# A mixture-of-experts tower on one core: 17 expert tiles listed ahead of the other 22, and the token permutation moved from TensorE's operands to VectorE

## The reference

```python
h = take(W.T, x) + b + positions                    # embedding
u = layernorm(h)
Bu = einsum(u, B_bar)                               # 64 complex states
xs = associative_scan(x_t = Lambda_bar * x_(t-1) + Bu_t)   # along a sequence
h = h + gelu(2 * real(einsum(xs, C_tilde)) + D * u)
v = layernorm(h)
logits = v @ router_w.T + router_b                  # 8 experts
w, e = softmax(top_k(logits, 2))
y_e = (silu(v @ fc1a_e.T + b1a_e) * (v @ fc1b_e.T + b1b_e)) @ fc2_e.T + b2_e
out = h + w_0 * y_(e_0) + w_1 * y_(e_1)
```

## Time and profile before

| | us |
|---|---|
| median of 3 runs | 197.66 |
| the profiled execution | 196.35 |
| its span, first to last instruction | 194.6 |
| PE busy / PE weight loads busy | 126.1 / 105.5 |
| DVE busy / ACT busy / POOL busy | 124.0 / 72.0 / 90.5 |

### The profile page before, as it was taken

How to read it: one execution, slowest core, us unless ns; L and a number is a source line. 1 busy time by engine, 2 the same in 40 slices (tenths; PEclk the granted TensorE clock), 3 DMA queues, 4 the chain that set the end, 5 groups by cost and what they waited for, 6 DMA issues and landing times.

```text
span 194.6 us, 3493 instructions
## 1 busy us (share of the span) xinstructions
PE 126.1 (65%) x784; PEld 105.5 (54%) x784; DVE 124.0 (64%) x478; ACT 72.0 (37%) x230; POOL 90.5 (46%) x117
## 2 busy tenths in 40 slices
PE   0000493969967948835230999999999999995000
PEld 0000323929826817715230888889888988894000
DVE  1838979599997498344530277777777677762082
ACT  2010633181271131141000665666556655663000
POOL 6787850000077375373671045556555565556100
PEclk9999998795896695765555599999999999999555
DMA  4221275050061061011012223333341011100493
GB/s 117 69 54 42 54 153 131 0 163 0 5 203 55 31 216 41 14 56 44 27 55 55 68 60 86 104 99 84 89 111 56 32 40 42 41 33 20 136 398 115
DMA packets 13445, 15.57 MB, mean 80 GB/s; under 512 B 3027, under 2 KB 9437, under 8 KB 13426
## 3 DMA queue, kind: packets, MB, share of 16 engines
q1 hardware_dynamic: 9474, 8.17, 15.8%
q0 software_dynamic: 2784, 5.28, 8.2%
q10 hardware_dynamic: 1168, 1.90, 2.8%
HBM read 9.53 MB, written 6.27 MB: 81 GB/s over the span
## 4 chain that ended last, share of the span: by engine, by line
PE 43%; DVE 26%; issue 14%; DMA 6%; POOL 4%; ACT 3%; DVEq 0%; POOLq 0%; SPq 0%; ACTq 0%
PE bank L902 8%; PE bank L908 7%; PE bank L918 7%; PE bank L791 5%; PE bank L894 4%; PE bank L793 4%; PE bank L792 4%; POOL sorted_rows L320 3%; PE bank L920 2%; DVE zst L486 2%; DMA yres<-results 2%; DVE ysum L635 1%; DVE res L638 1%; DVE zin L485 1%; DVE zrot L489 1%
## 5 line engine op out<-in xcount | busy, mean ns | idle before, releaser
L330 POOL DMA_INDIRECT results<-ysb,dest x39 | 38.4, 984 | 38.9 <-ACT ysb L737 24.4
L320 POOL DMA_INDIRECT sorted_rows<-rows,slot x32 | 31.3, 977 | 44.8 <-DVE slot L533 36.3
L608 DVE SCALAR_TENSOR_TENSOR act_h<-bank,bias_t,sil 128x128 f32<-128x128 f32 x78 | 23.8, 347 | 16.3 <-PE bank L908 15.9
L599 DVE COPY w1b<-w_sb 128x512 f32 x39 | 24.2, 621 | 11.9 <-issue 11.9
L717 ACT COPY xT<-bank 128x128 f32<-128x128 f32 x39 | 10.4, 266 | 43.1 <-issue 21.6
L902 PE MATMUL bank<-xT,w1b 128*128 128x128 f32 x156 | 24.9, 284 | 0.0
L725 ACT ACTIVATE sil<-bank,bias_t 128x128 f32<-128x128 f32 x78 | 24.4, 364 | 0.9 <-PE bank L902 0.9
L908 PE MATMUL bank<-xT,w1b 128*128 128x128 f32 x156 | 24.4, 280 | 0.0
L918 PE MATMUL bank<-w_sb,act_h 128*128 x156 | 23.9, 276 | 0.1
L902 PEld LDWEIGHTS bank<-xT,w1b 128*128 128x128 f32 x156 | 23.4, 212 | 0.3 <-issue 0.3
L908 PEld LDWEIGHTS bank<-xT,w1b 128*128 128x128 f32 x156 | 21.3, 198 | 0.0
(11 more groups left out here) (191 smaller groups left out, 215.7 us busy)
## 6 DMA issues: line engine op xcount, KB each, us to landing
w_sb<-w_all SPq DMA_DIRECT2D x8, 384.0 KB
xt<-sorted_rows SPq DMA_DIRECT2D x39, 65.0 KB, 1.9
yres<-results SPq DMA_DIRECT2D x4, 256.0 KB, 4.4
yres<-results ACTq DMA_DIRECT2D x4, 256.0 KB, 4.9
results<-ysb,dest POOLq DMA_INDIRECT x39
sorted_rows<-pad SPq DMA_DIRECT2D x1, 520.0 KB, 5.9
sorted_rows<-rows,slot POOLq DMA_INDIRECT x32
out<-res SPq DMA_DIRECT2D x2, 256.0 KB, 2.5
```

The source lines that it names most:

```text
L320: gp.indirect_dma_start(sorted_rows[:, :], bass.IndirectOffsetOnAxis(ap=slot[:, k, t:t + 1], axis=0), rows[:, k, t, :], None).then_inc(s_s ...
L330: gp.indirect_dma_start(results[:, :], bass.IndirectOffsetOnAxis(ap=dest[:, i:i + 1], axis=0), ysb[i][:, :], None, bounds_check=bound, oob ...
L599: v.tensor_copy(w1b[i % 3][:, :], w_sb[:, bass.ds(at, 2 * HID)]).then_inc(s_wb, 1)
L608: v.scalar_tensor_tensor(act_h[i % 2][:, q], ps_l[i % 2][:, q], bias_t[:, 2 + c, i:i + 1], sil[i % 2][:, q], ALU.add, ALU.mult).then_inc(s ...
```

## The change

1. **Two lists of tiles.** Once three of the four groups have been sorted, 24 tiles' worth of rows are there, and at least 24 - 7 = 17 full tiles of 128 rows whatever the routing is. `EARLY` = 17 such tiles get their own table (`early_counts`, `early_owners`, `early_table`, `early_bias`), which waits for nothing of group 3. SP loads them when the scatters of groups 0 to 2 have landed (`s_scat` is now one semaphore per group). The other 22 tiles (`LATE`) get theirs afterwards (`late_table`), from the full counts less what the first list has done. The scatter of an early tile's result takes its row numbers straight from `xt`.
2. **Token permutation on DVE.** `turn_u` writes its tiles side by side, `outputs` reads `zrot` and `uT` without a step, and DVE's four multiplications in `scan(g)` read PSUM (L510 and L512 of the changed kernel) or write SBUF (L519, L520) with a step of 128 elements instead.
3. **Start.** `root_h` is set among POOL's first constants, and ACT fills `decay` after it has copied `bbarT`.

```diff
-CHUNKS = [0, 2, 4] + list(range(8, NTILES, 4)) + [NTILES]
+EG = 3
+EARLY = EG * GT * K - (NE - 1)
+LATE = NTILES - EARLY
+CHUNKS = [0, 2, 4, 8, 12] + list(range(EARLY, NTILES - 3, 4)) + [NTILES]
...
+            sp.wait_ge(s_table_a, 2)
+            held = [tile_row(i) for i in range(AHEAD)]
+            for g in range(EG):
+                sp.wait_ge(s_scat[g], 16 * K * GT)
+            for i in range(EARLY):
+                load(i, held[i] if i < AHEAD else tile_row(i))
             sp.wait_ge(s_table, 2)
-            early = [tile_row(i) for i in range(AHEAD)]
+            held = [tile_row(EARLY + i) for i in range(AHEAD)]
             sp.wait_ge(s_pads, 16)
-            sp.wait_ge(s_scat, 16 * K * NT)
-            for i in range(NTILES):
-                load(i, early[i] if i < AHEAD else tile_row(i))
+            for g in range(EG, NG):
+                sp.wait_ge(s_scat[g], 16 * K * GT)
+            for i in range(EARLY, NTILES):
+                load(i, held[i - EARLY] if i < EARLY + AHEAD else tile_row(i))
...
             gp.memset(ident[:, :], 0.0).then_inc(s_pool, 1)
+            gp.memset(root_h[:, :, :], 0.0).then_inc(s_rooth, 1)
...
             gather(1)
-            gp.memset(root_h[:, :, :], 0.0).then_inc(s_rooth, 1)
...
+            def in_time(ap):
+                return ap.rearrange("p (b q j) -> p b q j", b=2, j=GT)
+
+            def by_tile(ap):
+                return ap.rearrange("p (j b q) -> p b q j", j=GT, b=2)
...
-                begin(v.tensor_tensor(per_seq(rot[:, 0, :]), per_seq(ps_v[:, :]), cos_b, ALU.mult))
+                begin(v.tensor_tensor(in_time(rot[:, 0, :]), by_tile(ps_v[:, :]), cos_b, ALU.mult))
...
-                v.tensor_tensor(per_seq(zrot[:, 0, :]), per_seq(zst[:, :]), cos_b, ALU.mult).then_inc(s_zrot, 1)
+                v.tensor_tensor(by_tile(zrot[:, 0, :]), in_time(zst[:, :]), cos_b, ALU.mult).then_inc(s_zrot, 1)
...
+            def early_counts():
+                begin(v.memset(done[:, :], 0.0))
+                begin(v.tensor_scalar(weight_e[:, :], weight_e[:, :], float((NE - 1) * WE), None, ALU.min))
+                dve.wait_ge(s_cnt_a, 1)
+                step(v.tensor_scalar(full_a, ps_tab_a[0:NE, 0:1], region_e[0:NE, :], 1.0 / P, ALU.subtract, ALU.mult))
+                step(v.tensor_scalar(full_a, full_a, -(P - 1) / (2.0 * P), MAGIC, ALU.add, ALU.add))
+                v.tensor_scalar(tiles_a[:, :], full_a, MAGIC, None, ALU.subtract).then_inc(s_tiles_a, 1)
...
             choose(2)
             find_slots(2)
+            early_counts()
             add_gelu(3)
+            early_owners()
             choose(3)
             find_slots(3)
+            early_table()
...
             expert_weights(0)
             expert_weights(1)
+            early_bias()
+            late_table()
...
             a.copy(bbarT[:, :, :].rearrange("p c s -> p (c s)"), ps_bT).then_inc(s_bbarT, 1)
+            act.wait_ge(s_radius, 1)
+            a.activation(decay[:, :].rearrange("p (b t) -> p b t", b=2),
...
-                z = zrot[:, :, :].rearrange("p c (q j) -> p c j q", j=GT)
...
-                    te.matmul(q, z[:, 0, j, :], cmat[:, 0, :], start=True, stop=False)
+                    te.matmul(q, zrot[:, 0, j * P:(j + 1) * P], cmat[:, 0, :], start=True, stop=False)
...
             outputs(3, 1)
+            pe.wait_ge(s_seen, EG)
+            te.matmul(ps_tab_a[0:NE, 0:1], seen[:, EG, :], ones_b[:, 0:1], start=True, stop=True).then_inc(s_cnt_a, 1)
+            pe.wait_ge(s_tiles_a, 1)
+            te.matmul(ps_tab_a[0:NE, 1:2], before[0:NE, 0:NE], tiles_a[:, :], start=True, stop=True).then_inc(s_begin_a, 1)
             turn_x(3)
             logits(3)
```

More of the change, by code:

```diff
@@ L535, in find_slots @@
                 dve.wait_ge(s_seen, g + 1)
+            start_a, end_a, base_a, cut_a = (tab_a[:, i:i + 1] for i in range(4))
+            full_a = tab_a[:, 4:5]
+            early_t = iota_t[0:NE, 0:EARLY]
+            def early_counts():
[5 more added lines that the diff above has]
+                v.tensor_scalar(tiles_a[:, :], full_a, MAGIC, None, ALU.subtract).then_inc(s_tiles_a, 1)
@@ L558, in _ @@
             find_slots(2)
+            early_counts()
             add_gelu(3)
+            early_owners()
             choose(3)
             find_slots(3)
-            last, count, tiles, start, end, rowbase = (tab[:, i:i + 1] for i in range(6))
-            begin(v.memset(last, float(P)))
-            step(v.memset(count, float(NTILES * P)))
-            begin(v.tensor_scalar(weight_e[:, :], weight_e[:, :], float((NE - 1) * WE), None, ALU.min))
-            dve.wait_ge(s_cnt, 1)
-            step(v.tensor_copy(tab[0:NE, 0:1], ps_set[0:NE, 0:1]))
@@ L569, in _ @@
-            step(v.tensor_tensor(tab[0:NE, 1:2], tab[0:NE, 0:1], region_e[0:NE, :], ALU.subtract))
-            begin(v.tensor_scalar(last, last, float(P), None, ALU.subtract))
-            step(v.tensor_scalar(tiles, count, P / 2 - 0.5, 1.0 / P, ALU.add, ALU.mult))
-            step(v.tensor_scalar(tiles, tiles, MAGIC, None, ALU.add))
-            step(v.tensor_scalar(tiles, tiles, MAGIC, None, ALU.subtract))
-            v.tensor_copy(tiles_b[:, :], tiles).then_inc(s_tiles, 1)
-            dve.wait_ge(s_begin, 1)
@@ L576, in _ @@
-            step(v.tensor_copy(start, ps_set[0:XE, 1:2]))
-            begin(v.tensor_tensor(end, start, tiles, ALU.add))
-            step(v.tensor_scalar(begun[:, :], iota_t[:, :], start, None, ALU.is_ge))
-            begin(v.scalar_tensor_tensor(owner[:, :], iota_t[:, :], end, begun[:, :], ALU.is_lt, ALU.mult))
-            step(v.scalar_tensor_tensor(rowbase, start, -float(P), region_e[:, :], ALU.mult, ALU.add))
-            step(v.tensor_scalar(rowval[:, :], iota_t[:, :], float(P), rowbase, ALU.mult, ALU.add))
@@ L650, in _ @@
             a.activation(cosw[:, :], cfrac[:, :], ACT.Sin, bias=prm[:, 6:7], scale=-2 * PI).then_inc(s_trig, 1)
-            act.wait_ge(s_radius, 1)
-            a.activation(decay[:, :].rearrange("p (b t) -> p b t", b=2),
-                         ktab[:, None, 0:SEQ].to_broadcast([P, 2, SEQ]), ACT.Identity,
-                         bias=col[:, 31:32], scale=0.0).then_inc(s_decay, 1)
             def normed_u(g):
@@ L700, in _ @@
             a.copy(bbarT[:, :, :].rearrange("p c s -> p (c s)"), ps_bT).then_inc(s_bbarT, 1)
+            act.wait_ge(s_radius, 1)
+            a.activation(decay[:, :].rearrange("p (b t) -> p b t", b=2),
+                         ktab[:, None, 0:SEQ].to_broadcast([P, 2, SEQ]), ACT.Identity,
+                         bias=col[:, 31:32], scale=0.0).then_inc(s_decay, 1)
             normed_u(1); copy_uT(1)
@@ L875, in _ @@
+            pe.wait_ge(s_w, 16 + 16 * NE)
+            pe.wait_ge(s_table_a, 2)
+            for c in range(4):
+                ins = te.matmul(ps_tab_a[:, at_bias + c * EARLY:at_bias + (c + 1) * EARLY],
+                                b1_sb[0:NE, c * P:(c + 1) * P], owner_a[:, :], start=True, stop=True)
+            ins.then_inc(s_biast_a, 1)
             pe.wait_ge(s_tiles, 1)
-            te.matmul(ps_set[0:XE, 1:2], before[0:XE, 0:XE], tiles_b[:, :], start=True, stop=True).then_inc(s_begin, 1)
+            te.matmul(ps_tab[0:XE, 1:2], before[0:XE, 0:XE], tiles_b[:, :], start=True, stop=True).then_inc(s_begin, 1)
@@ L881, in _ @@
             pe.wait_ge(s_table, 2)
             for c in range(4):
[L883 to L888 removed]
+                te.matmul(ps_tab[:, at_bias + c * LATE:at_bias + (c + 1) * LATE], b1_sb[:, c * P:(c + 1) * P],
+                          owner[:, :], start=True, stop=True)
@@ L890, in turn @@
+            te.matmul(ps_tab[:, at_dup:at_dup + LATE], ones_e[:, :], rowdup[:, :], start=True, stop=True).then_inc(s_biast, 1)
             def turn(i):
```

165 lines of the change are left out of this document (113 added, 52 removed).

## The result

The kernel after takes 192.51 us in the median, against 197.49 for the kernel before on the same chip: 5.0 us less. The ratio is 0.9721, 95% interval 0.9677 to 0.9765, which would be 5.5 us gained. The forecast was 190.2 us and a gain of 7.5. The profiled execution took 191.59 us, with a span of 189.1 against 194.6.

What follows compares the result with a forecast made beforehand. Bounds: PE's outputs in groups 0, 2 and 3, DVE in group 1, then the hole and PE's expert loop. 2.9 + 3.1 - 2.4 - 1.2 + 5.1 = 7.5 off 197.66 gives 190.2 us; range 186.6 to 194.6.

Steps and rivals of the forecast that it cites:

- Start: DVE's 2.93 us wait for `root_h` near 10.29 us goes: 2.9 us gained, bounds 2.2 to 4.0.
- PE's operands: Contiguous operands speed up PE's `outputs` passes in groups 0, 2 and 3: 3.1 us gained, bounds 1.6 to 8.8.
- POOL's burst: POOL's small constants at 24 to 27 us meet the scan: about 1 us more gained, or some 0.7 less.
- The clock shares: Second halves of groups 0, 2 and 3 at the higher PE clock 74%, 10% and 44% of the time.
- the weight loads: PE's weight loads of `outputs`, 330 ns in the median with a step, would take 137 to 230 ns.
- DVE's stepped operands: Each of 16 scan multiplications on DVE pays 0.15 us for its step: 2.4 us lost, bounds 0 to 4.5.
- Rival 3: Each stepped element costs DVE a second one, 0.54 us per operation, 8.6 in all: 196.4 us; chance 0.11.
- The new wait in group 3: `early_counts` ahead of `add_gelu(3)` on DVE waits for a late PE matmul: 1.2 us lost, bounds 0.9 to 1.5.
- The hole: Last slots to PE's first expert turn shrinks from 14.4 to 9.3 us: 5.1 gained, bounds 4.0 to 6.5.
- The critical list: Before the experts, the late table on DVE and PE ends last, not the data; tile 0 waits loaded.
- the clock rise sooner: PE works right up to the expert loop, so its clock rises sooner; the hole's upper bound, 6.5 us, assumes this.

Runs made afterwards that it cites:

- permutation only: Kernel before with the token permutation alone (DVE's four multiplications step through memory, PE's transposes and outputs read contiguously): 196.49 us, ratio 0.9932.
- lists only: Kernel before with the two lists of tiles alone, start and permutation as before: 190.62 us, ratio 0.9732.
- counts late: Kernel after with `early_counts` put behind group 3's residual additions on DVE: 189.75 us, ratio 0.9664.
- start only: Kernel before with both start edits alone (`root_h` set ahead of POOL's constants, ACT's `decay` moved): 196.66 us, ratio 0.9916.
- the combination with half the permutation: Kernel after with later tile loads held for group 3's scatters, late counts, POOL's constants early; `zrot` written contiguously, PE reading it stepped: 185.43 us, ratio 0.9466.
- the one with the full permutation: Kernel after with fourth and later tile loads held for group 3's scatters, counts late, POOL's constants ahead of groups 2 and 3's gathers: 186.03 us, ratio 0.9491.

## Why the prediction was right, and where its terms were off

The direction, the critical path after the change and the range held; the gain was 5.0 (by the profile 5.45) and not 7.5. Two terms, PE's operands and DVE's, came out near their size by luck. Its steps in order:

**Start, 2.9 forecast, 1.9 measured.** The first residual addition at 10.23 and the product 3.06 us earlier were as told. The prediction then let POOL's burst do DVE 1 us of good or 0.7 of harm by slower operations. What came instead were signals 0.85 and 1.11 us late. In the six traces with the early start and without them A is 23.7 to 24.0, some 3.9 us gained, close to the upper bound of 4.0. The slower operations are there too, but small: in all six, group 0's scan stands beside POOL's last constants and takes 0.3 to 0.4 us longer than the other groups', its second write into `zrot` 1.22 us against 1.03 in three of them.

**PE's operands, 3.1 forecast; 3.6 measured** in permutation only, 4.4 and 5.0 in the other two pairs. The gains per pass were right: 0.02 us at the lower level and 0.12 at the higher. Which passes run at which level was not, and the sum came near by luck. Groups 0 to 3 were forecast at 1.4, 0, 0.6 and 1.0 and gave 0.4, 0.4, 1.4 and 1.4. The clock shares were taken from before and did not stay, as the stretches after show. Wrong too were the weight loads, forecast at 137 to 230 ns, whose median stayed at 333.

**DVE's stepped operands, 2.4 forecast, 2.5 measured, by the wrong route.** Not 16 operations at 0.15, but eight at 0.27 to 0.35 and eight at nothing. Rival 3's 0.54 compares with 0.35 and with half the instructions. The Trainium skill, "SBUF — State Buffer" (Door 1: The DMA port swizzle, the note on cachelines), has a penalty for each access that crosses to a new 16-byte line, and here the trace agrees in kind for SBUF: 0.35 written, 0.39 read, per 512 elements. What it says of non-contiguous patterns in PSUM it says of matmuls, which the prediction left out; for DVE's reads the trace has 686 and 681 ns, no cost. The Trainium skill, "VectorE: DVE Perf Modes" (Mode 1× (REGULAR) — the baseline), says that odd strides and PSUM operands all work in this mode and that it gives one result per cycle. That both go together holds in these traces for PSUM alone.

**The new wait in group 3, 1.2 forecast, 1.0 measured** in lists only: from the last multiplication's end to the second addition 7.87 us against 6.86. Putting the counts behind gave back 0.7 in the profile of "counts late" and 1.1 by the ratios.

**The hole, 5.1 forecast, 4.1 measured in after, 5.8 in five traces.** This is the term that was mis-sized, in both directions. The critical list was the right one: the turn stands behind the late table products and finds its tile loaded, 8.8 us after the start of the last `slot` in after and in lists only alike, where the prediction had 9.3 + 0.23. So the working was too careful by 0.7 us. But in after the signals of the last product and of the turn come 2.1 and 1.8 us late, and the prediction had no term for signals. The table of the stages has the same loss in C, 1.1 us for the signal of the logits' last product. What D gains E partly gives back: D and E together fall from 20.4 us to 17.2 in after, 3.2 gained, and to 15.3 to 15.5 in the five traces, 4.9 to 5.1 gained.

**What was counted at nothing.** E is 0.9 longer. The prediction had the clock rise sooner, since PE works up to the loop. It rises later: counted from the first product after 5.3 us in after and 3.2 in before, and four passes take 0.85 us as long as it is low. The stretch from the first product to the first result, first before, then after (columns as in the earlier trace rows):

```profile
107.90:112.65 4.75, 4.75 (x28) 4.56 (x28) 1.99 (x8) 3.29 (x10) 0.00 (x0) 0.66 0.26 60
102.29:107.92 5.63, 5.63 (x27) 5.29 (x28) 2.44 (x8) 3.11 (x9) 0.00 (x0) 0.53 0.26 52
```

G is 0.8 shorter: the end comes 3.4 us after the issue of the last store in before, start only and permutation only, and 2.4 us after it in all kernels with two lists. In before the last landing stands 1.0 us behind its neighbours. Why, no run shows.

Sum by the profile: 1.9 + 0.7 - 1.1 + 4.1 - 0.9 + 0.8 = 5.5. The parts alone give 1.7 + 1.3 + 5.2 = 8.2 us, near the forecast's 7.5, but the 5.2 comes from the chip without late signals and the other two do not. In after the late signals account for 2.0 us in A (before has 0.9 itself), 1.1 in C and 1.7 in D (11.5 against 9.8).

## What to carry to other kernels

Move an engine's list earlier and ask what else is then in the air: a signal can be the last thing to come even where its work has long been done, and the profile calls it "remote" or "unknown queue". Try issuing loads that nothing needs yet only after a burst of scatters that others wait through. Here one such wait took 1.7 us out of D on one chip, of which 0.8 came back in E, and gave nothing on another. So measure it on more than one chip. Let DVE take a permutation where it reads PSUM, and check each stepped operand in SBUF by itself, since there it costs half as much again.

## What the runs showed of the hardware

- A DVE multiplication of 128x512 fp32 with a step takes 0.68 us when the step is in the PSUM operand, 1.04 when it is in the SBUF result (step 512 bytes), 1.09 when it is in both SBUF operands (step 16 bytes); contiguous 0.69.
- While POOL issues indirect DMAs one behind the other, 1.25 us apart, and in the 2 us or so behind the last, signals of DVE and PE were late by 0.5 to 2.3 us in all ten traces of the first chips, also an engine's signals to itself. Up to the first expert product none was in the four of the last chip.
- A contiguous fp32 pass of 128x128 follows the one before it by 0.213 us at the lower clock level and 0.112 at the higher; with a step of 16 bytes in its weights by 0.233 at either.
- SP's loads from `sorted_rows` that fall into such a stretch followed each other by 1.4 to 2.9 us in six traces on two chips at least, in place of 1.1, and by 1.1 on the last chip.
- The best kernel is the combination with half the permutation: 0.9466 of the time of before, 185.43 us; the one with the full permutation is the same within the intervals.
